# Dealing out TensorE's large products among the small ones of a scan step (adaLN block: RWKV-6 attention and FP4 feed-forward)

## What is computed

```python
sx = shift(x) - x;  m = tanh((x + sx * maa_x) @ tm_w1)
xw, xk, xv, xr, xg = [x + sx * (maa[i] + m_i @ tm_w2[i]) for i in range(5)]
r, k, v, g = xr @ Wr, xk @ Wk, xv @ Wv, silu(xg @ Wg)
w = exp(-exp(time_decay + tanh(xw @ td_w1) @ td_w2))
def step(state, r_t, k_t, v_t, w_t):            # over 4096 tokens
    a = outer(k_t, v_t)
    y = r_t @ (state + u * a)
    return w_t * state + a, y
out = (headnorm(y) * ln_w + ln_b) * g @ Wo
```

## Time and profile before

| | us |
|---|---|
| median of 3 runs | 4235.33 (4228.73 to 4249.51) |
| the profiled execution, its own time | 4212.4 |
| its span, first to last instruction | 4210.4 |
| TensorE matmul busy in it | 3699.2 (88%) |
| VectorE busy in it | 3525.5 (84%) |
| ScalarE, GpSimd busy | 1608.1, 1142.4 |

### The profile page before, as it was taken

One profiled execution on the slowest core, in us unless ns is written; L12 is line 12 of the kernel. 1 busy time (PEld: TensorE's weight loads), 2 busy tenths in 40 slices (PEclk: granted clock), 3 DMA queues, 4 the chain that ended last, 5 costly groups with the idle time before them and its releaser, 6 DMA issues. The chain is left out here.

```text
span 4210.4 us, 155629 instructions
## 1 busy us (share of the span) xinstructions
PE 3699.2 (88%) x65992; PEld 2513.7 (60%) x65992; DVE 3525.5 (84%) x7798; ACT 1608.1 (38%) x3173; POOL 1142.4 (27%) x736
## 2 busy tenths in 40 slices
PE   4989898888988988888898943699999999999998
PEld 3767677676776767767677732355555555455554
DVE  4888878878887887878888859799999999999997
ACT  2434344343443534434344313233333333333333
POOL 1122212222212221222222215333333333333332
PEclk7999999999999999999999976799999999999999
DMA  4000000000000000010000030011101111111110
GB/s 116 13 26 25 24 28 18 29 23 24 28 19 28 23 24 28 19 33 18 24 28 19 18 125 10 23 31 36 34 31 39 31 39 31 39 31 34 36 31 31
DMA packets 73617, 133.45 MB, mean 32 GB/s; under 512 B 13248, under 2 KB 14016, under 8 KB 72896
## 3 DMA queue, kind: packets, MB, share of 16 engines
q1 hardware_dynamic: 72896, 123.13, 9.2%
HBM read 89.56 MB, written 33.55 MB: 29 GB/s over the span
## 5 line engine op out<-in xcount | busy, mean ns | idle before, releaser
L764 POOL TENSOR_TENSOR raw_up<-raw_up,raw_gate 128x1024 f32<-128x1024 f32 x128 | 312.3, 2440 | 1077.4 <-DVE raw_up L814 1077.4
L932 DVE COPY_PREDICATED Am<-pick,banks 128x64 f32<-128x64 uint8 (+2 forms) x1792 | 461.4, 257 | 127.7 <-DVE Am L932 12.4
L1647 PE MATMUL fbank<-dT,hqT 128*128 128x512 f16 x2112 | 488.8, 380 | 20.8 <-ACT hqT L1564 20.8
L1635 PE MATMUL fbank<-gT,xqT 128*128 128x464 f16 (+1 forms) x2304 | 490.9, 363 | 11.4 <-issue 6.6
L1635 PE MATMUL fbank<-uT,xqT 128*128 128x464 f16 (+1 forms) x2304 | 487.7, 361 | 0.0
L530 PE MATMUL banks<-raw_up,raw_gate 128*128 128x256 f32 x2048 | 457.5, 382 | 1.8 <-DVE xxx L827 1.8
L530 PEld LDWEIGHTS banks<-raw_up,raw_gate 128*128 128x128 f32 x2048 | 385.5, 191 | 53.7 <-issue 2.1
L775 POOL TENSOR_TENSOR yrs<-yvar,neg_half 128x32 f32<-128x32 f32 x32 | 174.0, 5437 | 819.8 <-DVE yvar L961 819.8
L1575 ACT ACTIVATE sil<-fbank,und 128x464 f32<-128x464 f32 (+1 forms) x192 | 124.0, 646 | 655.0 <-PE fbank L1635 655.0
L1635 PEld LDWEIGHTS fbank<-gT,xqT 128*128 128x128 f16 x2304 | 225.6, 98 | 248.3 <-issue 12.6
L1635 PEld LDWEIGHTS fbank<-uT,xqT 128*128 128x128 f16 x2304 | 225.5, 98 | 231.1 <-issue 0.4
(11 more groups left out here) (235 smaller groups left out, 7686.9 us busy)
## 6 DMA issues: line engine op xcount, KB each, us to landing
raw_scale<-in_L_attn_x SPq DMA_DIRECT2D x32, 512.0 KB, 3.7
xres<-in_L_attn_x SPq DMA_DIRECT2D x32, 512.0 KB, 3.6
x_after_attention<-xres SPq DMA_DIRECT2D x32, 512.0 KB, 3.6
xl<-x_after_attention SPq DMA_DIRECT2D x64, 256.0 KB, 2.8
xr<-x_after_attention SPq DMA_DIRECT2D x64, 256.0 KB, 2.7
out<-xr SPq DMA_DIRECT2D x64, 256.0 KB, 2.0
raw_gate<-in_L_ffn_w_gate SPq DMA_DIRECT2D x1, 2816.0 KB, 11.4
raw_up<-in_L_ffn_w_up SPq DMA_DIRECT2D x1, 2816.0 KB, 18.9
```

The source lines that it names most:

```text
L764: nc.gpsimd.tensor_tensor(xf[:, j % NXF].rearrange("p g b t -> p (g b) t"), xf[:, j % NXF].rearrange("p g b t -> p (g b) t"), hT[:, :, :, ...
L932: nc.vector.copy_predicated(dst, mask, src).then_inc((done or A_step).sem, 1)
L1635: last = nc.tensor.matmul(GU[2 * pair + t][:, 0:w], xqT[:, u, a, g, :], W[:, b_, g, lo_:hi_], start=(k == 0), stop=(k == 3 * G - 1))
L1647: last = nc.tensor.matmul(DN[1 - u][:], hqT[:, a, kk, :], dT[:, b_, kk, :], start=(first and kk == 0), stop=(end and kk == KF - 1))
```

## The change

No product is added or removed. `pe_scores`, `pe_y`, `pe_td1` and `pe_g` take the part that they are to issue as an argument, and `pe_body` deals them out. In the steps n = 1 to 7 a step has four places for large products: in the middle of the scores (0), between the scores and the outer product (1), behind the outer product (2), and in the middle of the products of y (3). Before, all large products of a step but the delta stood at place 2.

```diff
             for n in range(1, 8):
+
+                def between(place):
+                    if do_w and n <= 3 and place < 3:
+                        pe_g(pe, c, n, ((0,), (1, 2), (3,))[place], do_p)
+                    if do_p and n == 4 and place < 3:
+                        pe_td1(pe, i, ((0,), (1, 2), (3,))[place])
+                    if do_f and n in (5, 6) and place < 2:
+                        pe_wo(pe, f, 0, (2 * (n - 5) + place,), do_p, do_w)
+                    if do_p and n == 6 and place == 2:
+                        pe_td2(pe, i)
+                    if do_f and n == 7:
+                        pe_wo(pe, f, 1, (place,), do_p, do_w)
                 if do_w:
-                    pe_scores(pe, c, n)
+                    pe_scores(pe, c, n, (0, 1))
+                between(0)
+                if do_w:
+                    pe_scores(pe, c, n, (2, 3))
+                between(1)
+                if do_w:
                     pe_outer(pe, c, n)
-                    if n <= 3:
-                        pe_g(pe, c, n, do_p)
-                if n == 4 and do_p:
-                    pe_td1(pe, i)
-                if n == 5 and do_f:
-                    pe_wo(pe, f, 0, (0, 1), do_p, do_w)
-                if n == 6 and do_f:
-                    pe_wo(pe, f, 0, (2, 3), do_p, do_w)
-                if n == 6 and do_p:
-                    pe_td2(pe, i)
-                if n == 7 and do_f:
-                    pe_wo(pe, f, 1, (0, 1, 2, 3), do_p, do_w)
+                between(2)
                 if do_w:
-                    pe_y(pe, c, n - 1)
+                    pe_y(pe, c, n - 1, (0, 1))
+                between(3)
+                if do_w:
+                    pe_y(pe, c, n - 1, (2, 3))
```

More of the change, by code:

```diff
@@ L421, in sp_body, with pe_scores @@
                 sp.dma_start(x1[:, tok(f), :].rearrange("b t n -> t b n"), xres[:]).then_inc(x1_stored.sem, 16)
-        def pe_scores(pe, c, n):
+        def pe_scores(pe, c, n, gs):
             b, q = divmod(n, Q)
             sc, scm = SC[n % 2], XB[n % 2]
-            if n == 0:
+            if gs[0] > 0:
+                pass
+            elif n == 0:
                 settled_after(pe, mod_done, (der, c), (ru_done, c), (m1_done, c), (k_done, c), (derk, c, 2))
@@ L430, in pe_scores @@
                 settled_after(pe, mod_done, (A_done, c, n - 1))
-            for g in range(G):
+            for g in gs:
                 X = (g * B + b) * Q + q
@@ L434, in pe_scores @@
                     nc.tensor.matmul(sc[d, g * NS:(g + 1) * NS], kvar[d, 0, g, b, 32 * q:32 * q + 32], rcol[d, X, 0:M1], start=True, stop=True)
-            for g in range(G):
-                X = (g * B + b) * Q + q
                 for d in HEADS:
@@ L450, in pe_outer, with pe_y @@
             last.then_inc(score_done.sem, 1)
-        def pe_y(pe, c, n):
+        def pe_y(pe, c, n, gs):
             b, q = divmod(n, Q)
-            if n == 0:
+            if gs[0] > 0:
+                pass
+            elif n == 0:
                 settled_after(pe, mod_done, (A_done, c, n + 1), (yT_done, c - 1))
@@ L467, in pe_y @@
                     last = nc.tensor.matmul(out, state[d, b, q, g, :], r32[d, X, :], start=False, stop=True)
-            last.then_inc(y_done.sem, 1)
+            if gs[-1] == G - 1:
+                last.then_inc(y_done.sem, 1)
         def pe_x(pe, i):
@@ L503, in xf_wait, with pe_td1 @@
             after(eng, xf_done_v, i) if j == 0 else after(eng, xf_done_p, i, j)
[L505 to L509, removed]
+        def pe_td1(pe, i, ks):
+            if ks[0] == 0:
+                xf_wait(pe, i, 0)
+                after(pe, mf_done, i)
+                after(pe, gu_done, i - 1)
+            for k in ks:
                 for b in range(B):
                     last = nc.tensor.matmul(SMALL[HALVES[b], 0:TC], w_td1[:, k, :], xf[:, 0, k, b], start=(k == 0), stop=(k == G - 1))
-            last.then_inc(td1_done.sem, 1)
+            if ks[-1] == G - 1:
+                last.then_inc(td1_done.sem, 1)
         def pe_td2(pe, i):
@@ L532, in pe_proj, with pe_g @@
                 last.then_inc(proj_done.sem, 1)
-        def pe_g(pe, c, g, do_p):
-            if g == 0:
+        def pe_g(pe, c, g, ks, do_p):
+            if ks[0] > 0:
+                pass
+            elif g == 0:
                 xf_wait(pe, c, NMIX - 1)
@@ L541, in pe_g @@
                 after(pe, gu_done, c, 1)
-            for k in range(G):
+            for k in ks:
                 last = nc.tensor.matmul(SMALL[:, (g % 2) * BT:(g % 2 + 1) * BT], w_g[:, k, g * P:(g + 1) * P],
                                         xf[:, NMIX - 1, k].rearrange("p b t -> p (b t)"), start=(k == 0), stop=(k == G - 1))
-            if g % 2:
+            if g % 2 and ks[-1] == G - 1:
                 last.then_inc(proj_done.sem, 1)
@@ L564, in pe_body @@
             if do_w:
-                pe_g(pe, c, 0, do_p)
+                pe_g(pe, c, 0, (0, 1, 2, 3), do_p)
                 pe_outer(pe, c, 0)
             for n in range(1, 8):
-                if do_w:
-                    pe_scores(pe, c, n)
-                    pe_outer(pe, c, n)
-                    if n <= 3:
-                        pe_g(pe, c, n, do_p)
-                if n == 4 and do_p:
-                    pe_td1(pe, i)
-                if n == 5 and do_f:
-                    pe_wo(pe, f, 0, (0, 1), do_p, do_w)
-                if n == 6 and do_f:
-                    pe_wo(pe, f, 0, (2, 3), do_p, do_w)
-                if n == 6 and do_p:
-                    pe_td2(pe, i)
-                if n == 7 and do_f:
-                    pe_wo(pe, f, 1, (0, 1, 2, 3), do_p, do_w)
+                def between(place):
[9 more added lines that the diff above has]
+                        pe_wo(pe, f, 1, (place,), do_p, do_w)
+                if do_w:
+                    pe_scores(pe, c, n, (0, 1))
[4 more added lines that the diff above has]
+                if do_w:
+                    pe_outer(pe, c, n)
+                between(2)
                 if do_w:
-                    pe_y(pe, c, n - 1)
+                    pe_y(pe, c, n - 1, (0, 1))
+                between(3)
+                if do_w:
+                    pe_y(pe, c, n - 1, (2, 3))
                 if n <= 5 and do_p:
@@ L589, in pe_body @@
             if do_w:
-                pe_y(pe, c, 7)
+                pe_y(pe, c, 7, (0, 1, 2, 3))
             if more:
@@ L599, in pe_body @@
                 pe_proj(pe, i, 3, lambda h: after(pe, ru_done, i, h + 1))
-                pe_scores(pe, i, 0)
+                pe_scores(pe, i, 0, (0, 1, 2, 3))
         def act_hT(act, i):
```

## The result

The changed kernel takes 4310.39 us (median of 4 runs, 4308.06 to 4326.35), the kernel before 4232.6 beside it; the ratio is 1.0184, 95% interval [1.0161, 1.0207]. That is 78 us slower, where the forecast was 84 (4319). So what follows explains 114 us between two executions, and the medians say that about 78 of them are typical.

A forecast was written before the change was run, and what follows sets the result against it. TensorE alone was taken to bound the tail and hand-over, both engines being tight in the scan. Wait 1.3, clock 1.2 and outer products 0.3 made 2.8 us in 30 passes, 84 us: 4319 us, range 4255 to 4372.

The forecast's parts named there:

- The stages: One loop pass cut in three where VectorE hands over: two bound by TensorE alone, in the scan both engines tight.
- The tail: From `dve_der_w` to the next chunk's first `dve_A`; TensorE busy 29.37 of 29.37 us, expected to stay 29.4.
- the hand-over: From the end of `dve_out(f, 0)` to `dve_der_w`; TensorE without gap; forecast 7 to 8.5 us instead of 5.1.
- The wait for `x1_done`: In step 7's scores: TensorE stands 2.4 to 3.4 us per full pass; pass 1.3 us longer (0.9 to 2.1).
- The clock: Behind the step 7 standstill the granted clock falls, costing 1.2 us a pass (0 to 1.7).
- The later outer products of steps 5 and 6: Two Wo products go ahead of each, and VectorE's `dve_A` waits: 0.3 us a pass (0 to 2).
- scan: From a chunk's first `dve_A` to the end of `dve_out(f, 0)`; 40.01 us, forecast 38 to 41.
- The switches: Between small and large products: 14 added runs a pass at 0.3 us, 4.2 us; 11 in the scan costed at 0.
- The sum: 1.3 + 1.2 + 0.3 = 2.8 us in each of 30 full passes, 84 us, median 4319 us.
- The signs: What the changed kernel's profile would show: `x1_done` waits of 70 to 100 us in 30 places, low clock, longer hand-over.
- Rival 3: Faster: code loading hides behind dealt-out products and scan gaps close, 27 us less, 4208; chance 0.08.
- Which standstills are code: TensorE's 7.86 us of scan standstill, releaser "issue", read as TensorE waiting for its instructions to load.

The follow-up runs named there:

- the large filler: Changed kernel plus four redundant products of 288 columns ahead of the wait for `x1_done` in step 7; 1.0066 of the kernel before.
- g alone: Kernel before with only g dealt out (steps 1 to 3, 6 added runs) and the scores in the new group-by-group order; 0.9972 of the kernel before.
- all but the second Wo: Changed kernel with the four Wo products of the second sequence together again behind the outer product of step 7; 1.0026 of the kernel before.
- the early `dve_out`: Changed kernel with VectorE issuing `dve_out` of the first sequence ahead of its step 6; 0.9848 of the kernel before, 4156.57 us against 4213.43.

## Why the prediction was right, point by point

- **The stages.** The tail and the hand-over go by TensorE alone. From the projections to the next first `dve_A` it is 29.8 us before and after, so the reading that VectorE's extra delay is absorbed there holds.
- **The wait for `x1_done`.** Forecast 2.4 to 3.4 us in each of 30 passes; measured 92.2 us in 30, 3.1 each. The chain behind it at full clock was forecast at 3.5 us to `dve_A` and 6.95 to `dve_der_w`; with the large filler it was 3.54 and 6.89. TensorE's part was forecast as 1.3 us a pass with 0.9 as the lower bound. The filled kernel has 6.27 us to the projections, where 5.35 stood before: 0.9. So the term measured 0.9 and was 0.4 us too large. Half of that is the average of two passes that I set it against (5.14), which lies below the mean of 29 (5.35).
- **The clock.** Forecast 1.2 us a pass, bounds 0 and 1.7. The filler gives back 1.7 us; the clock is low in 30 of 30 hand-overs, for 4.1 us on average. Another 0.5 us of low clock a pass did lie in the standstill, as I had allowed for, but in 10 of the 30 passes the clock stayed low for 4.75 to 6.5 us, longer than in the stretch that I had priced. The term was mis-sized by 0.5 us, to its bound.
- **The later outer products of steps 5 and 6.** Forecast 0.3 us (0 to 2). VectorE's waits at these steps went from 0.20 and 0.31 to 0.81 and 0.95 us, and the experiment with g alone against that with all but the second Wo gives 0.5% for td1 and the first Wo, 0.8 us a pass. But the whole scan did not grow by that much for this reason: with the large filler, at waits no shorter (0.82 and 1.12), it is 39.38 us, 0.18 more than before, and with g alone it is 38.41. As far as single executions tell, what is lost at steps 5 and 6 is mostly won back in the steps before.
- **The switches.** 0.3 us for each run: the lone Wo product took 1.06 us, as 0.86 + 0.2 says. That the 11 in the scan do not lengthen the pass by their time is borne out by the runs with g alone and with the early `dve_out`: they are faster than before. They do cost TensorE work: it is busy 66.05 us a pass before, 67.51 with the 6 runs of g and 69.24 with 11 (a small part of that is low clock), 0.24 and 0.29 us for each, and its "issue" standstills shrink from 8.12 to 6.31 and 4.13 us a pass. The reason that the prediction gave, that a weight load runs beside products in flight only where the row groups differ, does not fit its own: the 32 records of the full array there each have a weight load of 0.19 us on the same row groups, and still take 0.215 us a record, so the loads run beside the products. The price of a switch rests on its measurement alone.
- **The sum.** By the medians, the kernel with the large filler is 0.66% over the kernel before, 28 us or 0.9 a pass, and the changed kernel another 1.18%, 50 us or 1.7 a pass. Together that is 2.6 us a pass, the measured 78 us, and it is the 0.9 of the wait and the 1.7 of the clock with next to nothing for the scan. The forecast 2.8 was 1.3 + 1.2 + 0.3: the wait 0.4 too large, the clock 0.5 too small, the scan 0.3 too large. Each lies within its bounds or at one of them, but that the total is off by only 6 us is partly luck, since the errors cancel. The single profiled execution shows 3.45 us a pass; it lies 16 us above its median and that of the kernel before 20 below, together 1.2 us a pass. Why single executions of one kernel differ by 20 us is open.
- **The signs.** The waits for `x1_done`, the scan, the clock and the missing wait of `dve_out(f, 1)` came as forecast. VectorE's wait at step 7 (5.23 us, forecast 3.4 to 5) and the hand-over (8.59, forecast 7 to 8.5) came out just over, which is the clock term again.
- **Rival 3.** Its mechanism is real: TensorE's standstills fell by half, and with VectorE's order changed as well the kernel is 1.5% faster than before. I priced it at 1.8 us a pass in VectorE's waits, and left out that the wait can be removed by VectorE's order. That 1.5% would have come from dealing out alone is not shown.
- **Which standstills are code.** The prediction read "issue" as instructions being loaded, and the traces bear it out. Seven such standstills make 7.8 of the 7.86 us of the scan in the earlier trace rows. In the attention of the kernel before, the trace has 212 of them, and 209 end between 1.1 and 1.7 us after a 16 KB packet of the instruction queue has landed (1.39 at the median); of moments picked at random, 11% do. The 1.53 us of the earlier trace rows, for instance, end at 1050.34, and a packet landed at 1048.90. In the changed kernel it is 149 of 151. No run changed the loading alone.

## What to carry to other kernels

Before work is moved forward on an engine that runs in order, look at the wait that it carries and at what then stands behind that wait: here a semaphore that had cost 2.6 us in all went ahead of the one product that the other engine needed next, and made most of the 78 us. When a good rearrangement loses, try to move the signal before undoing it: four lines on VectorE turned 1.018 into 0.985. And the length of a standstill of TensorE may not be its whole price: here one of 3.1 us on average was followed by half clock in 30 of 30 passes, 1.7 us more. Redundant large products in it were worth their time; 72 small ones ran past the wait and were not.

## What the runs showed of the hardware that I had not expected

- Redundant work paid: four products of 288 columns in the wait took the low clock from 30 hand-overs to 1 and 1.2% off the time.
- Dealing large products out among small ones more than halved TensorE's "issue" standstills, from 253 to 119 us, although it adds 14 switches of some 0.3 us to each pass.
- The low clock does not go by the length of the single wait alone: with the second Wo back in place (waits for `dve_out` of 1.4 us on average) it came in 19 of 30 hand-overs, with only the second Wo dealt out (1.3 us) in 6. What tells these two apart is open.
- TensorE can stand still for its own instructions: 253 us of the attention before the change, in standstills that end some 1.4 us after a 16 KB packet of instructions has landed.
